# Attention messages moved from VectorE to GpSimd in a graph network on one core

## The chip, the cores and the metric

The kernel runs on one core of a Trainium2 chip. The metric is the device time in microseconds (us). A core has TensorE (PE in the profile), VectorE (DVE), ScalarE (ACT), GpSimd (POOL) and SyncE (SP), which issues DMAs here.

## The reference, cut to what matters

A graph of 12,500 nodes with 32 features and 400,000 edges goes through four layers, each followed by a layer norm: a weighted sum over neighbours, an attention layer, two hops of a normalized sum, and a convolution. The change touches the attention layer:

```python
hp = jnp.einsum('nf,hfo->hno', h, w)             # 4 heads
e = a_src[:, src] + a_dst[:, dst] + fc_b[0]
e = jax.nn.leaky_relu(e, negative_slope=0.2)
seg_max = jax.ops.segment_max(e.T, src, num_segments=n)
e = jnp.exp(e - seg_max.T[:, src])
seg_sum = jax.ops.segment_sum(e.T, src, num_segments=n)
att = e / seg_sum.T[:, src]
msg = att[:, :, None] * hp[:, dst, :]
agg = jax.vmap(lambda m: jax.ops.segment_sum(m, src, num_segments=n))(msg)
out = agg.mean(axis=0) + bias
```

The kernel sums exp(score) times the far node's row, and exp(score) itself (a 33rd column of ones), per source node and head; it divides and projects afterwards. Everything is float32.

## The kernel before, in words

The layers run one after the other as stages; each ends in a barrier of all engines. The attention stage (`attend`) has two paths; the inputs take the bounded one, in which a bound on the scores that was computed earlier takes the place of the maximum. GpSimd's `If` holds only the bounded path.

Edges, sorted by source node, are worked in groups of 512 (128 partitions x `PER` = 4). There are 880 groups in `SRC_PASSES` = 110 turns of `SRC_DEEP` = 8 groups; the first and the last turn are written out and the others are a loop on each engine. Each engine runs its own instruction list, and semaphores tie them. For a group s:

- SP loads the far nodes' rows into `far[s]` (8 buffers, 80 KB each) once `far_free[s]` has been raised.
- VectorE forms `local_node` (L1825, 128x4) and from it `one_hot` (L1830: 512 columns, a comparison of the iota with the local node numbers, both in SBUF).
- TensorE transposes the one-hot (`turn_hot`, L1941); ScalarE copies the result to SBUF (L1983).
- GpSimd copies the node's terms into `b_node` (L2007, 128x8).
- TensorE multiplies the two (`spread_terms`, L1951), which gives each edge its node's terms in PSUM.
- VectorE makes the score in four short operations of 16 columns: `raw_score` (L1836, PSUM and SBUF in), `leaky_score` (L1841, the same SBUF tile as both inputs), `less_bound` (L1845, SBUF and PSUM in), `cap_score` (L1850, SBUF).
- ScalarE takes the exponent into `b_share` (L1987).
- VectorE forms the message (L1855): `far` (33 columns, spread over 4 heads) times `b_share` (spread over 33 columns), both in SBUF, 528 columns out. `free_far` then waits for it and raises `far_free`.
- TensorE sums the messages per node (`sum_nodes`, L1960) into one of two PSUM buffers, and VectorE adds the result to `k.attention` (`accumulate`, L1871).

The work is staggered. In its iteration s VectorE does, in this order: one_hot(s+1), local_node(s+2), messages(s-2), raw_score(s-1), free_far(s-2), leaky_score(s-1), accumulate(s-4), less_bound(s-1), cap_score(s-1). TensorE does turn_hot(s), spread_terms(s-1), sum_nodes(s-3). ScalarE does copy_hot(s), the exponent of s-1. GpSimd only copies node terms, up to four groups ahead (its copy waits for the spread_terms of four groups before). Scores, shares, messages, turned one-hots and node terms have `SLOTS` = 4 buffers each.

Of the kernel before, what the change touches and what calls it, by code (L numbers as in the profile page):

```python
# [20 lines left out]
ALU = mybir.AluOpType  # L21
# [7 lines left out]
HEADS = 4  # L29
# [7 lines left out]
SLOTS = 4  # L37
# [49 lines left out]
SRC_DEEP = 8  # L87
SRC_PASSES = TURNS["by_src"] * SLOTS // SRC_DEEP
# [25 lines left out]
def spread(ap, axis, n):  # L114

    ap = ap.unsqueeze(axis)
    shape = list(ap.shape)
    shape[axis] = n
    return ap.broadcast_to(shape)
# [8 lines left out]
def loop(engine, first, end):  # L128

    return engine.bass.Fori(first, end, engines=[engine.engine], head_slot={engine.engine: 0})  # L130
# [7 lines left out]
def turns(engine, count, one_turn):  # L138

    one_turn(0, True, False)  # L140
    with loop(engine, 1, count - 1) as i:
        one_turn(i, False, False)
    one_turn(count - 1, False, True)
# [1402 lines left out]
def attend(nc, k):  # L1546
# [4 lines left out]
    W = F + 1  # L1551

    def turn(i, slot, of):
        return i * (SRC_DEEP // of) + slot // of + 1

    with stage(nc, k) as ctx:
        def sb(n, shape, dt, count):
            return [ctx.enter_context(nc.sbuf_tensor(f"att_{n}{s}", shape, dt)) for s in range(count)]

        def sem(n, count):  # L1560
            return [k.sem(f"att_{n}{s}") for s in range(count)]

        far = sb("far", [P, PER, FAR], F32, SRC_DEEP)
# [9 lines left out]
        gathered, far_free = sem("gathered", SRC_DEEP), sem("far_free", SRC_DEEP)  # L1573
# [14 lines left out]
        b_share = sb("b_share", [P, PER, HEADS], F32, SLOTS)  # L1588
        b_message = sb("b_message", [P, PER, HEADS * W], F32, SLOTS)
# [7 lines left out]
        b_score_ready, b_share_ready = sem("b_score_ready", SLOTS), sem("b_share_ready", SLOTS)  # L1597
        b_message_ready, b_part_ready = sem("b_message_ready", SLOTS), sem("b_part_ready", SLOTS)
# [216 lines left out]
        def bounded_vector(dve):  # L1815
            steps = Steps(dve, own)
            step, wait = steps.step, steps.wait
            step(dve.memset(k.attention[:], 0.0))
            wait()
            for c in range(2):  # L1820
                dve.sem_inc(part_free[c], 1)

            def local_node(i, s):
                dve.wait_ge(gathered[s % SRC_DEEP], (i + s // SRC_DEEP + 1) * 16)
                return step(dve.tensor_scalar(b_local[s % SLOTS][:], far[s % SRC_DEEP][:, :, SRC_AT],  # L1825
                                              first_node[:, bass.ds(i * SRC_DEEP + s, 1)], None, ALU.subtract))

            def one_hot(s):

                dve.tensor_tensor(b_hot[s % SRC_DEEP][:], spread(k.iota[:], 1, PER),  # L1830
                                  spread(b_local[s % SLOTS][:], 2, P), ALU.is_equal).then_inc(b_hot_ready[s % SLOTS], 1)


            def raw_score(i, s):
                dve.wait_ge(b_terms_spread[s % SLOTS], turn(i, s, SLOTS))
                return step(dve.tensor_tensor(b_score[s % SLOTS][:, 0], b_terms[s % 2][:, :, 0:HEADS],  # L1836
                                              far[s % SRC_DEEP][:, :, W:W + HEADS], ALU.add))

            def leaky_score(s):
                score = b_score[s % SLOTS]  # L1840
                return step(dve.scalar_tensor_tensor(score[:, 1], score[:, 0], 0.2, score[:, 0], ALU.mult, ALU.max))  # L1841

            def less_bound(s):
                score = b_score[s % SLOTS]
                return step(dve.tensor_tensor(score[:, 0], score[:, 1], b_terms[s % 2][:, :, HEADS:2 * HEADS],  # L1845
                                              ALU.subtract))

            def cap_score(s):
                score = b_score[s % SLOTS]
                dve.tensor_scalar(score[:, 1], score[:, 0], 0.0, None, ALU.min).then_inc(b_score_ready[s % SLOTS], 1)  # L1850

            def messages(i, s):
                b = s % SLOTS
                dve.wait_ge(b_share_ready[b], turn(i, s, SLOTS))
                dve.tensor_tensor(  # L1855
                    b_message[b][:].rearrange("p j (h w) -> p j h w", h=HEADS),
                    spread(far[s % SRC_DEEP][:, :, 0:W], 2, HEADS), spread(b_share[b][:], 3, W),
                    ALU.mult).then_inc(b_message_ready[b], 1)

            def free_far(i, s):  # L1860

                dve.wait_ge(b_message_ready[s % SLOTS], turn(i, s, SLOTS))
                dve.sem_inc(far_free[s % SRC_DEEP], 1)

            def bins(first, n):
                return bins_of(nc, mybir.EngineType.DVE, k, "by_src", first, n)

            def accumulate(i, s, at):
                dve.wait_ge(b_part_ready[s % SLOTS], turn(i, s, SLOTS))
                sums = k.attention[:, bass.ds(at * (HEADS * W), HEADS * W)]  # L1870
                return step(dve.tensor_tensor(sums, sums, part[s % 2][:, 0:HEADS * W], ALU.add))  # L1871

            def one_group(i, s, first, last, at, n_local):

                if not (last and s == SRC_DEEP - 1):
                    if n_local:
                        wait(n_local)
                    one_hot(s + 1)
                n_local = None
                if not (last and s >= SRC_DEEP - 2):  # L1880
                    n_local = local_node(i, s + 2)
                if not (first and s < 2):
                    messages(i, s - 2)
                scored = not (first and s < 1)
                if scored:
                    n_raw = raw_score(i, s - 1)
                if not (first and s < 2):
                    free_far(i, s - 2)
                if scored:
                    wait(n_raw)  # L1890
                    n_leaky = leaky_score(s - 1)
                if at is not None:
                    n_added = accumulate(i, s - 4, at)
                if scored:
                    wait(n_leaky)
                    n_less = less_bound(s - 1)
                    wait(n_less)
                    dve.sem_inc(b_terms_read[(s - 1) % SLOTS], 1)
                    cap_score(s - 1)
                if at is not None:  # L1900
                    wait(n_added)
                    dve.sem_inc(part_free[s % 2], 1)
                return n_local

            def one_turn(i, first, last):
                steps.restart()
                at = [None] * 4 + [*bins(0, SRC_DEEP - 4)] if first else bins(i * SRC_DEEP - 4, SRC_DEEP)
                n_local = None
                for s in range(SRC_DEEP):
                    n_local = one_group(i, s, first, last, at[s], n_local)  # L1910
                wait()

            local_node(0, 0)
            wait()
            one_hot(0)
            local_node(0, 1)
            wait()
            turns(dve, SRC_PASSES, one_turn)

            steps.restart()  # L1920
            i, s = SRC_PASSES - 1, SRC_DEEP - 1
            messages(i, s - 1)
            wait(raw_score(i, s))
            wait(leaky_score(s))
            wait(less_bound(s))
            dve.sem_inc(b_terms_read[s % SLOTS], 1)
            cap_score(s)
            at = bins(i * SRC_DEEP + SRC_DEEP - 4, 4)
            for n in range(4):
                wait(accumulate(i, s - 3 + n, at[n]))  # L1930
                dve.sem_inc(part_free[n % 2], 1)
                if n == 0:
                    messages(i, s)

        def bounded_tensor(pe):
            def turn_hot(i, s):
# [60 lines left out]
            exponents(SRC_PASSES - 1, SRC_DEEP - 1)  # L1997

        def bounded_gpsimd(pool):
            def one_turn(i, first, last):  # L2000
                at = bins_of(nc, mybir.EngineType.Pool, k, "by_src", i * SRC_DEEP, SRC_DEEP)
                for s in range(SRC_DEEP):
                    b = s % SLOTS

                    if not (first and s < SLOTS):
                        pool.wait_ge(b_terms_spread[b], turn(i, s, SLOTS) - 1)
                    pool.tensor_copy(b_node[b][:], k.node_terms[:, bass.ds(at[s] * (2 * HEADS), 2 * HEADS)]  # L2007
                                     ).then_inc(b_node_ready[b], 1)

            turns(pool, SRC_PASSES, one_turn)  # L2010

        def bounded(engine):
            return engine.value_load(k.bounded[0:1, 0:1], min_val=0, max_val=1) == 1
# [633 lines left out]
```

## Time and profile before

| what | value |
|---|---|
| median of 3 runs | 25015.46 us (25014.8 to 25022.9) |
| span of the profiled execution | 25016.3 us |
| attention stage, first local_node to last accumulate | 9084.1 to 11346.7 us |
| busy in it: TensorE, VectorE, ScalarE, GpSimd | 2130.6, 1934.4, 629.1, 377.0 us of 2262.0 |

The profiled execution has no other time than its span, which lies 0.8 us above the median of the runs. The page gives busy time per engine over the whole span; since the stages have different limits, the shares that count are those of the attention stage, read from windows and from its timeline.

### The profile page before, as it was taken

Reading aid. Unit: us, or ns where it says so; the run is one execution under the profiler, and the core shown is the slowest. Engines: PE = TensorE matmul, PEld = TensorE weight load, DVE = VectorE, ACT = ScalarE, POOL = GpSimd, SP = SyncE. Lnnn points to the kernel's source line nnn. Section 1 sums busy time; section 2 is a strip of 40 time slices with the busy share of each in tenths; the row PEclk is TensorE's granted clock in tenths of the full one; section 3 lists DMA queues with packets and bytes.
Section 4 is the critical chain, followed back from the end, with each engine's and each line's share of the span. In section 5 each row is a group of like instructions: output and inputs, shape, how many; then the busy total and the mean of one; then the engine's idle time right before and its main releaser. Section 6 shows DMA issues by size and latency. Waiting matters only on the chain. (4 is left out here: it accounts for less than half of the span.)

```text
span 25016.3 us, 315397 instructions
## 1 busy us (share of the span) xinstructions
PE 12737.2 (51%) x63351; PEld 12045.4 (48%) x63352; DVE 12424.7 (50%) x30310; ACT 5405.7 (22%) x16758; POOL 17008.4 (68%) x17867
## 2 busy tenths in 40 slices
PE   0333333344444469994333333333333588888887
PEld 0333333333333359994333333333333577777777
DVE  2377731211111148883222222222222699999999
ACT  6522222200000012220000000000000255555554
POOL 1777777677777741114777776777777677777777
PEclk8555555555555579995555555555555688888888
DMA  1111112332333311110000002000000222222223
GB/s 51 16 16 15 15 17 17 22 70 69 69 69 68 69 45 32 32 32 15 13 13 13 13 13 15 13 13 13 13 13 13 32 43 43 43 43 43 43 43 41
DMA packets 2491356, 794.50 MB, mean 32 GB/s; under 512 B 1959280, under 2 KB 2282065, under 8 KB 2490323
## 3 DMA queue, kind: packets, MB, share of 16 engines
q0 software_dynamic: 517120, 331.99, 9.2%
q1 hardware_dynamic: 1624386, 242.42, 6.0%
q10 hardware_dynamic: 349748, 219.11, 3.5%
q14 instruction: 84, 0.69, 0.0%
q8 instruction: 18, 0.29, 0.0%
HBM read 699.58 MB, written 93.71 MB: 32 GB/s over the span
## 5 line engine op out<-in xcount | busy, mean ns | idle before, releaser
L999 POOL DMA_INDIRECT hop_far<-hop_rows,hop_index x6464 | 6097.5, 943 | 2188.6 <-issue 2188.3
L1061 PE MATMUL hop_part<-hop_far,hop_hot 128*128 128x32 f32 x12928 | 2926.7, 402 | 5268.4 <-DVEq L1046 5268.4
L1061 PEld LDWEIGHTS hop_part<-hop_far,hop_hot 128*128 128x128 f32 x12928 | 2817.9, 330 | 5377.2 <-DVEq L1046 5377.2
L781 POOL DMA_INDIRECT weighted_far<-in_x_dram,weighted_rows x3232 | 3346.7, 1035 | 1505.4 <-issue 980.0
L1131 POOL DMA_INDIRECT rows_by_src<-push_row,push_index x3232 | 3094.7, 958 | 996.3 <-issue 985.0
L2255 POOL DMA_INDIRECT conv_far<-conv_rows x3232 | 3066.4, 949 | 949.9 <-issue 758.5
L1013 DVE TENSOR_TENSOR hop_hot<-hop_iota,local_of_edge 128x1024 f32<-128x1024 f32 x808 | 989.5, 1225 | 5035.4 <-DMA hop_far<-hop_rows,hop_index 3650.2
L2361 PE MATMUL conv_radial_a<-radial,conv_hidden 128*128 128x256 f32 x6464 | 2747.6, 513 | 634.6 <-DVE conv_products_b L2493 566.9
L865 PE MATMUL weighted_total<-weighted_message,weighted_hot 128*128 128x33 f32 x6464 | 1542.8, 404 | 2852.9 <-ACT weighted_message L887 2788.2
L1181 PE MATMUL push_near<-far_rows_sb,push_turned 128*128 x6464 | 1683.6, 436 | 2369.5 <-DVE push_turned L1158 2369.1
L865 PEld LDWEIGHTS weighted_total<-weighted_message,weighted_hot 128*128 128x128 f32 x6464 | 1438.3, 328 | 2958.2 <-issue 2958.2
L1181 PEld LDWEIGHTS push_near<-far_rows_sb,push_turned 128*128 128x128 f32 x6464 | 1569.0, 327 | 2484.0 <-issue 2483.9
L2361 PEld LDWEIGHTS conv_radial_a<-radial,conv_hidden 128*128 128x128 f32 x6464 | 1803.6, 327 | 697.7 <-issue 629.7
L2362 PEld LDWEIGHTS conv_radial_b<-radial,conv_hidden 128*128 128x128 f32 x6464 | 1910.6, 330 | 138.7
L986 ACT COPY hop_index<-source_of_edge 128x8 int32 (+1 forms) x808 | 158.7, 197 | 7965.3 <-PE hop_part L1061 7868.5
L2362 PE MATMUL conv_radial_b<-radial,conv_hidden 128*128 128x128 f32 x6464 | 1781.1, 363 | 0.0
L1166 DVE TENSOR_TENSOR push_index<-push_moved,push_trash 128x4 int32<-128x4 f32 x808 | 132.6, 164 | 3230.6 <-DMA rows_by_src<-push_row,push_index 3229.9
L1021 DVE TENSOR_TENSOR sums<-sums,hop_part 128x32 f32 x6464 | 1213.9, 188 | 923.1 <-issue 94.2
L2007 POOL COPY att_b_node<-node_terms 128x8 f32 x880 | 377.5, 429 | 1893.7 <-PE att_terms_ps L1951 969.9
L2493 DVE TENSOR_TENSOR conv_products_b<-conv_radial_b,conv_pair 128x1536 f32<-128x1536 f32 x808 | 1538.1, 1904 | 0.0
L2410 DVE TENSOR_REDUCE conv_sum_b<-conv_products_b 128x96 f32<-128x1536 f32 x808 | 1531.4, 1895 | 0.0
L887 ACT ACTIVATE weighted_message<-weighted_far,weighted_rows 128x32 f32<-128x32 f32 x3232 | 772.6, 310 | 2627.0 <-DMA weighted_far<-in_x_dram,weighted_rows 2626.8
(256 smaller groups left out, 22490.9 us busy)
## 6 DMA issues: line engine op xcount, KB each, us to landing
push_line<-local_by_group ACTq DMA_DIRECT2D x808, 256.0 KB
hop_far<-hop_rows,hop_index POOLq DMA_INDIRECT x6464
conv_weights<-weight_by_group SPq DMA_DIRECT2D x808, 128.0 KB, 3.0
att_far<-rows_by_src SPq DMA_DIRECT2D x880, 80.0 KB
weighted_far<-in_x_dram,weighted_rows POOLq DMA_INDIRECT x3232, 2.4
push_place<-place_by_dst SPq DMA_DIRECT2D x3232, 0.5 KB
rows_by_src<-push_row,push_index POOLq DMA_INDIRECT x3232
conv_rows<-edges_by_dst SPq DMA_DIRECT2D x3232, 4.0 KB
```

Source lines behind the costliest of these rows:

```text
L781: pool.indirect_dma_start(far[s][:, j, :], None, table, bass.IndirectOffsetOnAxis(ap=rows[s][:, j, 0:1].bitcast(I32), axis=0)).then_inc(ga ...
L865: last = pe.matmul(total[:].rearrange("p n c -> p (n c)")[:, bass.ds(at[s % SLOTS * HALVES + j // COLUMNS], width)], hot[s][:, j, :], mess ...
L999: pool.indirect_dma_start(far[q][:, j, :], None, table, bass.IndirectOffsetOnAxis(ap=index[q][:, j:j + 1], axis=0)).then_inc(gathered[q], 16)
L1021: return steps.step(dve.tensor_tensor(sums, sums, part[q % 2][:, j * F:(j + 1) * F], ALU.add))
L1061: last = pe.matmul(part[q % 2][:, j * F:(j + 1) * F], hot[q][:, j, :], far[q][:, j, :], start=True, stop=True)
L1131: pool.indirect_dma_start(k.rows_by_src, bass.IndirectOffsetOnAxis(ap=index[s][:, j:j + 1], axis=0), row[s][:, j, :], None).then_inc(writt ...
L1181: last = pe.matmul(near[:, b, j * FAR:(j + 1) * FAR], turned[b][:, :, j], k.far_rows[:].rearrange("p b w -> p (b w)")[:, bass.ds(at[b * HA ...
L2255: pool.indirect_dma_start(far[s][:, j, :], None, k.conv_dram, bass.IndirectOffsetOnAxis(ap=rows[s][:, j, 0:1].bitcast(I32), axis=0)).then_ ...
L2361: pe.matmul(radial_a[:, c, j, :], hidden[c][:, :, j], k.radial[:, 0:256], start=True, stop=True)
L2362: last = pe.matmul(radial_b[:, c, j, :], hidden[c][:, :, j], k.radial[:, 256:384], start=True, stop=True)
L2410: return step(dve.tensor_reduce(sum_b[s % 2][:].rearrange("p j o u -> p (j o u)"), products_b[:].rearrange("p j o u m -> p (j o u) m"), AX ...
L2493: dve.tensor_tensor(products_b[:].rearrange("p j o u m -> p (j o u m)"), spread(radial_b[:, c], 2, 3), spread(pair[s][:].rearrange("p j o ...
```

## The change

VectorE no longer forms the messages nor frees the loaded rows. GpSimd does both, in its own iteration s after the copy of the node terms: first free_far(s-3), then messages(s-2). Since VectorE's order no longer protects the message buffer, GpSimd also waits for the sum_nodes that read the buffer four groups before. In VectorE's list the two calls are simply gone; the rest keeps its order.

```diff
--- bounded_vector
-            def messages(i, s):
-                b = s % SLOTS
-                dve.wait_ge(b_share_ready[b], turn(i, s, SLOTS))
-                dve.tensor_tensor(
-                    b_message[b][:].rearrange("p j (h w) -> p j h w", h=HEADS),
-                    spread(far[s % SRC_DEEP][:, :, 0:W], 2, HEADS), spread(b_share[b][:], 3, W),
-                    ALU.mult).then_inc(b_message_ready[b], 1)
-            def free_far(i, s):
-                dve.wait_ge(b_message_ready[s % SLOTS], turn(i, s, SLOTS))
-                dve.sem_inc(far_free[s % SRC_DEEP], 1)
...
-                if not (first and s < 2):
-                    messages(i, s - 2)
...
-                if not (first and s < 2):
-                    free_far(i, s - 2)
--- bounded_gpsimd
+            def messages(i, s, first=False):
+                b = s % SLOTS
+                pool.wait_ge(b_share_ready[b], turn(i, s, SLOTS))
+                if not (first and s < SLOTS):
+                    pool.wait_ge(b_part_ready[b], turn(i, s, SLOTS) - 1)
+                pool.tensor_tensor(
+                    b_message[b][:].rearrange("p j (h w) -> p j h w", h=HEADS),
+                    spread(far[s % SRC_DEEP][:, :, 0:W], 2, HEADS), spread(b_share[b][:], 3, W),
+                    ALU.mult).then_inc(b_message_ready[b], 1)
+            def free_far(i, s):
+                pool.wait_ge(b_message_ready[s % SLOTS], turn(i, s, SLOTS))
+                pool.sem_inc(far_free[s % SRC_DEEP], 1)
             def one_turn(i, first, last):
...
                     pool.tensor_copy(b_node[b][:], ...).then_inc(b_node_ready[b], 1)
+                    if not (first and s < 3):
+                        free_far(i, s - 3)
+                    if not (first and s < 2):
+                        messages(i, s - 2, first)
             turns(pool, SRC_PASSES, one_turn)
+            i, s = SRC_PASSES - 1, SRC_DEEP - 1
+            messages(i, s - 1)
+            messages(i, s)
```

The last two messages, which VectorE formed after its loop, move to the end of GpSimd's list as well.

## Rows read from the trace of the kernel before

**Rows 1.** The page: the span; TensorE's clock in 40 slices, in tenths.

```profile
span 25016.3 us, 315397 instructions
...
PEclk8555555555555579995555555555555688888888
```

**Rows 2.** Windows: us, busy us (count) per engine, TensorE clock, DMA share, GB/s.

```profile
9084.00:11346.00 2262.00, 2130.56 (x17600) 2071.31 (x17600) 1934.41 (x7039) 629.10 (x1761) 376.96 (x876) 0.98 0.13 32
...
9090.00:9100.00 10.00, 10.00 (x49) 10.00 (x48) 6.81 (x24) 2.40 (x7) 0.57 (x3) 0.50 0.09 23
22000.00:22100.00 100.00, 83.30 (x375) 77.81 (x373) 100.00 (x202) 51.33 (x142) 78.02 (x78) 0.87 0.23 43
```

**Rows 3.** Groups by line, stage 9084 to 11346: busy us, mean ns | idle before.

```profile
L1855 DVE TENSOR_TENSOR att_b_message<-att_far,att_b_share 128x528 f32<-128x528 f32 x880 | 616.2, 700 | 0.7 <-ACT att_b_share L1987 0.6
...
L2007 POOL COPY att_b_node<-node_terms 128x8 f32 x876 | 377.0, 430 | 1884.4 <-PE att_terms_ps L1951 969.9 <-PE att_hot_ps L1951 914.5
```

**Rows 4.** Timeline, VectorE: start us, us, engine line op [idle before <-releaser].

```profile
10215.30 0.17 DVE L1850 TENSOR_SCALAR att_b_score<-att_b_score 128x16 f32<-128x16 f32 x1
10216.62 0.69 DVE L1830 TENSOR_TENSOR att_b_hot<-iota,att_b_local 128x512 f32<-128x512 f32 x1 [1.15 <-DVE att_b_score L1845]
...
10219.02 0.69 DVE L1830 TENSOR_TENSOR att_b_hot<-iota,att_b_local 128x512 f32<-128x512 f32 x1
10219.64 0.22 DVE L1825 TENSOR_SCALAR att_b_local<-att_far,first_node_by_src 128x4 f32<-128x4 f32 x1
10219.77 0.69 DVE L1855 TENSOR_TENSOR att_b_message<-att_far,att_b_share 128x528 f32<-128x528 f32 x1
10220.39 0.16 DVE L1836 TENSOR_TENSOR att_b_score<-att_terms_ps,att_far 128x16 f32<-128x16 f32 x1
10220.61 0.17 DVE L1841 SCALAR_TENSOR_TENSOR att_b_score<-att_b_score 128x16 f32<-128x16 f32 x1
10220.76 0.29 DVE L1871 TENSOR_TENSOR attention<-attention,att_part 128x132 f32 x1
10220.97 0.16 DVE L1845 TENSOR_TENSOR att_b_score<-att_b_score,att_terms_ps 128x16 f32<-128x16 f32 x1
10221.28 0.18 DVE L1850 TENSOR_SCALAR att_b_score<-att_b_score 128x16 f32<-128x16 f32 x1
10221.43 0.69 DVE L1830 TENSOR_TENSOR att_b_hot<-iota,att_b_local 128x512 f32<-128x512 f32 x1
```

**Rows 5.** The same, the next turn's first one-hot.

```profile
10237.02 0.69 DVE L1830 TENSOR_TENSOR att_b_hot<-iota,att_b_local 128x512 f32<-128x512 f32 x1 [1.15 <-DVE att_b_score L1845]
```

**Rows 6.** Timeline, TensorE: two groups and the turn's boundary.

```profile
10211.67 0.60 PE L1941 MATMUL att_masked_ps<-ident,att_masked 128*128 128x128 f32 x4
...
10214.01 0.60 PE L1941 MATMUL att_masked_ps<-ident,att_b_hot 128*128 128x128 f32 x4
10214.45 0.96 PE L1951 MATMUL att_hot_ps<-att_b_node,att_b_turned 128*128 128x8 f32 x8
...
10217.37 0.66 PE L1941 MATMUL att_masked_ps<-ident,att_b_hot 128*128 128x128 f32 x4 [0.79 <-DVE att_b_hot L1830]
```

**Rows 7.** Timeline, GpSimd: the node copies.

```profile
10215.57 0.19 POOL L2007 COPY att_b_node<-node_terms 128x8 f32 x1 [1.79 <-PE att_hot_ps L1951]
10218.99 0.19 POOL L2007 COPY att_b_node<-node_terms 128x8 f32 x1 [3.23 <-PE att_terms_ps L1951]
10221.61 0.55 POOL L2007 COPY att_b_node<-node_terms 128x8 f32 x1 [2.44 <-PE att_hot_ps L1951]
```

**Rows 8.** GpSimd's only long elementwise operation: ns min/median/max.

```profile
L2275 POOL TENSOR_TENSOR conv_folded_a<-conv_products_a x808: 1253/1266/1289, 19724.8 to 24968.7; 128x512 f32<-128x512 f32 x162
```

**Rows 9.** Timeline, ScalarE: the share after the capped score at 10221.28.

```profile
10221.49 0.21 ACT L1987 ACTIVATE att_b_share<-att_b_score 128x16 f32<-128x16 f32 x1 [1.72 <-DVE att_b_score L1850]
```

**Rows 10.** Register loads, ns min/median/max, GpSimd's queue.

```profile
L633 POOLq TENSOR_LOAD <-listed x110: 562/566/765, 9070.2 to 11313.1; - x110
```

**Rows 11.** Waits of the DMA queue: us in total, times, longest.

```profile
SPq L1612 <- DVEq L1863: 1679.5, 859, 3.8
```

More of the change, by code:

```diff
@@ L1886, in one_group @@
                     n_raw = raw_score(i, s - 1)
-                if not (first and s < 2):
-                    free_far(i, s - 2)
-                if scored:
                     wait(n_raw)
@@ L1921, in bounded_vector @@
             i, s = SRC_PASSES - 1, SRC_DEEP - 1
-            messages(i, s - 1)
             wait(raw_score(i, s))
@@ L1931, in bounded_vector @@
                 dve.sem_inc(part_free[n % 2], 1)
-                if n == 0:
-                    messages(i, s)
         def bounded_tensor(pe):
```

## The prediction

> **What bounds the kernel now.** I first read the span and the page's slices, which tell where the attention stage lies, by TensorE's clock, which reaches full speed (2.4 GHz) there alone [rows 1]. Windows give the stage 2262 us with TensorE 94% and VectorE 86% busy, GpSimd 17% [rows 2]. So two engines are near their limit, and only the order of instructions tells which one ends last. VectorE's timeline decides it: one group takes 10221.43 - 10219.02 = 2.41 us, and inside a turn VectorE never idles [rows 4]. TensorE needs 10214.01 - 10211.67 = 2.34 us for a group when it runs without a gap [rows 6]. VectorE is the bound by 0.07 us a group only, and at the boundary of each turn it adds 1.15 us of register loads and branch, in which TensorE soon stands too (0.79 us idle) [rows 4, 6]. A turn of eight groups is 10237.02 - 10216.62 = 20.40 us [rows 4, 5]; 110 turns are 2244 us, and the cold start is the rest of the stage.
>
> **What leaves VectorE.** The message is 880 x 0.70 us = 616 us of busy time [rows 3]. From start to start it takes 10220.39 - 10219.77 = 0.62 us out of a group [rows 4], so VectorE alone would need 1.79 us. free_far costs VectorE nothing visible. If nothing else changed, TensorE would be the bound at once, and the most that can be won inside a turn is 0.07 us a group; what more there is lies at the boundary.
>
> **What comes to GpSimd.** Its message is not in the trace. The nearest row is its own 128x512 addition of two SBUF tensors, 1.27 us (1.25 to 1.29) [rows 8]; by columns, 528/512 x 1.27 = 1.31 us. Below, it could be VectorE's 0.70 us [rows 3], above twice the 1.31 (2.6), if the two spread operands cost extra; I take 1.31, the same engine with the same kind of operation. With a node copy of 0.19 us, the waits (it wakes 10215.57 - (10214.45 + 0.96) = 0.16 us behind its releaser [rows 6, 7]) and one register load of 0.57 us a turn [rows 10], GpSimd needs some 1.8 us a group. It has 2.4. By busy time alone nothing speaks against the move.
>
> **What the two engines do to each other.** The node copy takes 0.19 us when VectorE's one-hot isn't under way, but 0.55 us when it starts inside one: started at 10221.61, it ends at 10222.16, 0.04 us after the one-hot that ran from 10221.43 to 10222.12 [rows 4, 7]. Its mean in the stage is 0.43 us [rows 3]. So GpSimd is kept off while VectorE runs an operation with two SBUF inputs. The trace has no case of the reverse, a long GpSimd operation with such a VectorE operation behind it: the only long one runs beside an operation that reads PSUM. I bound the reverse: at least nothing, at most the whole rest of the GpSimd message. I take the whole, since what keeps one engine off for a whole operation looks like one thing that both need, held until the operation ends.
>
> The Trainium skill ("SBUF — State Buffer", section "Who interferes with whom") says the same and more: the port pair that the two share is an exclusive lock, taken for a whole instruction by whoever is first, wanted by a VectorE operation with two SBUF inputs (against a GpSimd operation that reads SBUF) and by the two-port modes, into which fp32 `tensor_scalar` can fall. The trace agrees for one direction (0.55 against 0.19 us); no run here shows the other. By that rule one-hot, leaky_score and perhaps local_node and cap_score would wait for a message, and raw_score, less_bound and accumulate, with one input in PSUM, would not.
>
> **The new cycle, step by step,** counted from the start of cap_score(s-1) [rows 4, 9]:
> - the one-hot starts at 0.15 and ends at 0.15 + 0.69 = 0.84; the share starts at 0.21 and is done at 0.42, so GpSimd finds the message(s-1) ready at about 0.6, inside the one-hot, and is held;
> - held like the copy, the message ends its own length, less the copy's, after the copy would: 0.84 + 0.04 + 1.31 - 0.19 = 2.00;
> - VectorE meanwhile does local_node and raw_score, and wants leaky_score(s) at 0.15 + 1.59 - 0.62 = 1.12. It has two SBUF inputs and must wait to 2.00. It ends between 0.05 and 0.17 later (its latency);
> - cap_score(s) starts 10221.28 - 10220.61 = 0.67 after leaky_score's start, 0.50 after its end: the cycle is 2.55 to 2.67 us;
> - if local_node wants the pair too, it adds up to its own 0.22 us, when it gets in first. Together 2.55 to 2.89 us; I take the middle, 2.72.
>
> The next message can't slip into a better gap, since its share comes only from the cap_score that the one-hot follows at once. So the pattern holds itself: the message falls behind the one-hot and in front of the leaky_score every time.
>
> At a turn's boundary the one-hot comes 10216.62 - 10215.30 = 1.32 after the cap_score [rows 4]. Then the message is first: 0.42 + 0.16 + 1.31 = 1.89, and the one-hot wants its start at 1.32 and waits 0.57. From the one-hot's start to cap_score, without the message, are 10221.28 - 10219.02 - 0.62 = 1.64 us: 1.89 + 1.64 = 3.5 us. GpSimd's own register load falls while it waits for a share.
>
> **Sum.** A turn: 7 x 2.72 + 3.5 = 22.54 us against 20.40, 2.14 more. 110 turns: 235 us. The later stages begin after a barrier, so all of it arrives at the end. On the profiled span: 25016 + 235 = 25251; the median of the runs is 1 us less: 25,250.
>
> **What costs nothing, and its cover.** The wait for the sum of four groups before: that sum lies more than two cycles back. Rows are freed a group later: SP's wait for far_free is what it mostly does (1680 us, longest 3.8) [rows 11], eight buffers still leave three cycles, over 7 us, for a load. accumulate and sum_nodes wait for a message that ends at 2.00, and TensorE wants it after its transposes and its spread of the next iteration, at about 2.3. Should the message be 0.3 us later than that, TensorE's summing would be late next. The scalar engine is unchanged. The two last messages cost about 1 us more, once.
>
> TensorE would have 2.34 us of work in 2.72 (86%). In the convolution, at 83% busy, its clock is granted at 0.87 of full speed [rows 2], against 0.98 here now; at the low level (1.2 GHz) it had no gap left in the stage's start [rows 2]. At 0.87 its group costs 2.34 / 0.87 = 2.69, just under the cycle. I count nothing for it in the middle and up to 0.1 us a group (90 us) in the upper end.
>
> **The rivals.**
> *No blocking of VectorE's operations, faster.* For it: GpSimd's copy at 10218.99 starts 0.03 us before the one-hot and neither is longer for it (0.19, 0.69) [rows 4, 7]; against: an operation of 8 columns may be out by then. Then TensorE is the bound: 8 x 2.34, plus at the boundary 0 to 0.3 us, since VectorE, now 0.6 us a group ahead, hides most of the 1.15. A turn of 18.9 saves 1.5, 110 turns 165 us: 24,850 (24,820 to 24,880). It decides by one thing: whether leaky_score starts before the message ends. With only the one-hot blocked it is the same case, since the VectorE cycle is then about 2.0.
> *The parts cancel.* leaky_score waits only for part of the message, because the message is shorter (below 1.1 us) or lets the 16 columns in. A cycle of 2.35 to 2.48 and a boundary of 3.5 give 20.0 to 20.9 a turn: no change, 25,015.
> *GpSimd becomes the bound.* The spread operands cost extra. Each 0.1 us on the message is 0.1 us on the cycle, 88 us on the kernel; at 2.6 us the cycle is 4.0: some 26,150. Against it: nothing in the row speaks of such a cost; the operands are in SBUF there too.
>
> **Chances.** Forecast (mutual blocking) 0.58; faster rival 0.23; cancelling 0.13; GpSimd the bound 0.06. The forecast's own range is 7 x 2.55 + 3.4 = 21.25 to 7 x 2.89 + 3.6 = 23.8 us a turn, 25,110 to 25,390, with the clock's share up to 25,420. The range over all reaches down into the faster rival, where TensorE's 2.34 sets a floor: 24,835 to 25,420. A change under 0.2% (50 us) can't be told from none here. A little of the forecast's lower end falls under that bound: faster 0.24, same 0.14, slower 0.62.
>
> **What would show it.** GpSimd's L2007 mean and its new message group: about 1.3 us alone, near 1.5 from its start where it begins inside a one-hot. VectorE: idle time or a longer duration at leaky_score (0.9 us a group), none at raw_score. One-hots 2.7 us apart and 3.5 at the boundary. TensorE idle 0.3 to 0.4 us a group and a granted clock under 0.98. The forecast is wrong if VectorE's waits sit on raw_score behind TensorE's spread (the faster rival), or if GpSimd shows no gap at all.

## The result, and the profile after

The changed kernel takes 25220.16 us (median of 4 runs, 25216.36 to 25225.3) against 25015.13 us, a ratio of 1.0081 (95% interval 1.0067 to 1.0096): slower by 205 us, where 235 us had been forecast. Its profiled execution has a span of 25223.6 us. The number is close, but by luck: the cost that the forecast was made of came to a third of its size, the clock, which it had put at nothing, cost more than that, and a third part wasn't foreseen.

The page after, its span and TensorE's granted clock in 40 slices, and three windows (columns as in [rows 2]): the attention stage, a usual turn of it, and a slow one:

```profile
span 25223.6 us, 316380 instructions
...
PEclk8555555555555579996555555555555688888888
```

```profile
9117.00:11555.00 2438.00, 2245.12 (x17600) 2182.38 (x17600) 2036.28 (x6160) 631.91 (x1761) 1272.46 (x1757) 0.93 0.12 29
10229.00:10250.00 21.00, 19.01 (x162) 18.36 (x160) 18.43 (x56) 5.58 (x16) 11.53 (x17) 1.00 0.13 31
10250.30:10275.90 25.60, 24.67 (x160) 24.48 (x160) 18.73 (x57) 6.08 (x16) 11.57 (x17) 0.73 0.10 26
```

The stage goes from 2262.6 us (9084.1 to 11346.7) to 2438.0 us, 175 us more. TensorE's clock in it falls from 0.98 to 0.93, and the third window shows where: a turn of 25.6 us with a clock of 0.73, in which TensorE is busy for 24.67 us, so it hardly waits. Of the 109 intervals from a turn's first one-hot to the next, 82 are about 21.07 us and 27 are 24.3 to 26.2 us. Before, most were 20.40 us and the others 20.7, but for the first, with the cold start in it (25.8).

The groups of the stage (columns as in [rows 3]), and VectorE's and GpSimd's timelines of one cycle, beside [rows 4]:

```profile
L1984 POOL TENSOR_TENSOR att_b_message<-att_far,att_b_share 128x528 f32<-128x528 f32 x880 | 1105.9, 1257 | 1174.1 <-ACT att_b_share L1966 1174.0
L1825 DVE TENSOR_SCALAR att_b_local<-att_far,first_node_by_src 128x4 f32<-128x4 f32 x880 | 835.5, 949 | 0.2 <-DVE attention L1818 0.2
...
L2001 POOL COPY att_b_node<-node_terms 128x8 f32 x877 | 212.6, 242 | 2.3 <-issue 2.3
```

```profile
10201.72 0.17 DVE L1850 TENSOR_SCALAR att_b_score<-att_b_score 128x16 f32<-128x16 f32 x1
10201.86 0.69 DVE L1830 TENSOR_TENSOR att_masked<-iota,att_b_local 128x512 f32<-128x512 f32 x1
10202.47 1.05 DVE L1825 TENSOR_SCALAR att_b_local<-att_far,first_node_by_src 128x4 f32<-128x4 f32 x1
10203.44 0.16 DVE L1836 TENSOR_TENSOR att_b_score<-att_hot_ps,att_far 128x16 f32<-128x16 f32 x1
10203.64 0.17 DVE L1841 SCALAR_TENSOR_TENSOR att_b_score<-att_b_score 128x16 f32<-128x16 f32 x1
10203.76 0.29 DVE L1858 TENSOR_TENSOR attention<-attention,att_part 128x132 f32 x1
10203.97 0.17 DVE L1845 TENSOR_TENSOR att_b_score<-att_b_score,att_hot_ps 128x16 f32<-128x16 f32 x1
10204.28 0.17 DVE L1850 TENSOR_SCALAR att_b_score<-att_b_score 128x16 f32<-128x16 f32 x1
10204.43 0.69 DVE L1830 TENSOR_TENSOR att_b_hot<-iota,att_b_local 128x512 f32<-128x512 f32 x1
```

```profile
10202.22 1.28 POOL L1984 TENSOR_TENSOR att_b_message<-att_far,att_b_share 128x528 f32<-128x528 f32 x1 [1.15 <-ACT att_b_share L1966]
10203.44 0.19 POOL L2001 COPY att_b_node<-node_terms 128x8 f32 x1
```

VectorE's local_node, 4 columns wide, took 0.22 us before and takes 1.05 us now. It starts at 10202.47, while the message runs, and ends at 10203.52, 0.02 us after the message (10202.22 + 1.28 = 10203.50). raw_score and leaky_score behind it have their usual lengths. The message itself is held too: its 1.28 us began inside the one-hot. It is so in the whole stage: 768 of the 880 local_nodes start inside a message, take 1.06 us (median) and end 0.02 to 0.03 us after it; the others take 0.22 us. From cap_score to cap_score the cycle is 10204.28 - 10201.72 = 2.56 us; it was 2.41.

A turn's boundary, VectorE first, then GpSimd:

```profile
10206.84 0.17 DVE L1850 TENSOR_SCALAR att_b_score<-att_b_score 128x16 f32<-128x16 f32 x1
10208.17 0.89 DVE L1830 TENSOR_TENSOR att_b_hot<-iota,att_b_local 128x512 f32<-128x512 f32 x1 [1.16 <-DVE att_b_score L1845]
...
10209.95 0.17 DVE L1850 TENSOR_SCALAR att_b_score<-att_b_score 128x16 f32<-128x16 f32 x1
...
10229.23 0.89 DVE L1830 TENSOR_TENSOR att_b_hot<-iota,att_b_local 128x512 f32<-128x512 f32 x1 [1.16 <-DVE att_b_score L1845]
```

```profile
10207.43 1.08 POOL L1984 TENSOR_TENSOR att_b_message<-att_far,att_b_share 128x528 f32<-128x528 f32 x1 [1.23 <-ACT att_b_share L1966]
```

Here VectorE is busy with its registers when the share is ready. The message starts with VectorE out of its way, takes 1.08 us to 10208.51, and now it is the one-hot (from 10208.17) that is longer, 0.89 in place of 0.69 us. From cap_score to cap_score these are 3.11 us, and the turn is 10229.23 - 10208.17 = 21.06 us.

TensorE in the slow turn, the first transposes of four groups (columns as in [rows 6]):

```profile
10255.41 1.06 PE L1920 MATMUL att_masked_ps<-ident,att_b_hot 128*128 128x128 f32 x4
...
10259.73 1.06 PE L1920 MATMUL att_masked_ps<-ident,att_b_hot 128*128 128x128 f32 x4
...
10269.04 0.60 PE L1920 MATMUL att_masked_ps<-ident,att_masked 128*128 128x128 f32 x4
...
10271.27 0.60 PE L1920 MATMUL att_masked_ps<-ident,att_masked 128*128 128x128 f32 x4
```

At the low clock level (1.2 GHz) a group takes 10259.73 - 10255.41 = 4.32 us, TensorE back to back. When the level returns to 2.4 GHz it catches up, still without a gap, at 10271.27 - 10269.04 = 2.23 us a group. This is its true floor; the 2.34 us of [rows 6] wasn't. Besides the one that the stage starts in, the record of the clock has 26 low stretches in the stage both before and after, but of 3.4 us each before (89 us in all) and of 10.2 or 13.7 us now (338 us).

Ahead of the stage lies one more difference. GpSimd's indirect DMAs there, before and after (ns min/median/max):

```profile
L1131 POOL DMA_INDIRECT rows_by_src<-push_row,push_index x3232: 954/958/1005, 4981.8 to 9060.8; - x191
```

```profile
L1131 POOL DMA_INDIRECT rows_by_src<-push_row,push_index x3232: 965/969/1013, 4979.0 to 9093.6; - x191
```

11 ns more for each of 3232, in a stage whose code is the same: 36 us, of which 33 arrive at the attention stage (9116.9 - 9084.1), since the first of these DMAs comes 3 us earlier. So the 207 us between the spans are 33 ahead of the stage, (21.07 - 20.40) x 110 = 74 us of longer cycles, and the remaining 101 us of slow turns, beyond what such turns cost before.

### The profile page after: what moved, and what is told of

Read it like the earlier page. It is cut to its first block and busy times, and to the rows that moved or that the text cites. A ratio compares the mean times of both kernels' runs of the same rounds, so it can differ in the third digit from the quotient of the medians.

```text
span 25223.6 us, 316380 instructions
## 1 busy us (share of the span) xinstructions
PE 12847.3 (51%) x63351; PEld 12154.6 (48%) x63352; DVE 12526.2 (50%) x29430; ACT 5409.5 (21%) x16758; POOL 17938.9 (71%) x18747
## 5 line engine op out<-in xcount | busy, mean ns | idle before, releaser
L1984 POOL TENSOR_TENSOR att_b_message<-att_far,att_b_share 128x528 f32<-128x528 f32 x880 | 1105.9, 1257 | 1174.1 <-ACT att_b_share L1966 1174.0
```

## The experiments

In the first eight runs of the table the kernel before takes 27,400 to 27,660 us, since the stages of indirect DMAs are longer there, before and after alike: the one ahead of attention takes 4803 us from its first to its last such DMA in before_again, for 4079 us in the trace before. The cause isn't known, and it isn't the chip as such: by the record fill_tensor ran on the chip of the first four, at 25,120 us. The attention stage isn't longer (2260.4 us in before_again). So these runs are compared by their ratio to the kernel before in the same series, and by the length of the attention stage; the microseconds of their expectations are to be read as differences from 25,015. The 11 ns cost nothing in them (4800 us in after_again, 4803 in before_again), so their ratios lack the 33 us.

| run | ratio (95% interval) | stage, us | usual turn, us | low clock, us |
|---|---|---|---|---|
| before_again | one run | 2260.4 | 20.40 | 92 |
| after_again | one run, +171 us | 2429.7 | 21.06 | 311 |
| local_first | 1.0034 (1.0021 to 1.0048) | 2365.7 | 20.71 | 256 |
| psum_ops_first | 0.9908 (0.9892 to 0.9925) | 2019.5 | 18.27 | 0 |
| after_psum | 0.9897 (0.9880 to 0.9913) | 1979.4 | 17.86 | 0 |
| before_psum | 0.9999 (0.9989 to 1.0009) | 2261.8 | 20.38 | 113 |
| psum_order | 0.9894 (0.9877 to 0.9910) | 1984.6 | 17.86 | 7 |
| half | 1.0002 (0.9992 to 1.0011) | 2256.8 | 20.43 | 0 |
| local_psum | 0.9902 (0.9885 to 0.9918) | 1979.3 | 17.86 | 0 |
| free_only | 0.9999 (0.9989 to 1.0009) | 2262.6 | 19.97 | 195 |
| pad | one run, -2 us | 2260.2 | 20.40 | 96 |
| fill_tensor | 1.0043 (1.0030 to 1.0057) | 2327.3 | 21.05 | 10 |

The stage runs from the first local_node's start to the last accumulate's end, the usual turn is the median from one turn's first one-hot to the next, and the low clock is the sum of the stretches at the low level in the stage, without the one of 13 to 26 us that it starts in.

**after_again and before_again: do the parts repeat?**

> The changed kernel once more, unchanged. Its trace showed three parts of the 207 us: cycles of 2.56 us instead of 2.40 (73 us), a turn of 25.6 us instead of 21.1 about every fourth turn, in which TensorE's clock is at its low level for 13.7 us (some 100 us), and 36 us in the stage before attention, where each of GpSimd's 3232 indirect DMAs takes 11 ns longer from start to start (1.274 against 1.263 us). Theory: all three belong to the kernel and repeat: span 25,205 to 25,235, the stage before at 1.274 us, about 26 low stretches of 10 to 14 us. Rival: the slow turns and the 11 ns are chance of one execution; then one or both are gone (25,080 to 25,190).

> The kernel before once more, unchanged. If the 11 ns belong to the change, GpSimd's indirect DMAs of the stage before attention stand at 1.263 us again; if they are chance of an execution, they may stand at 1.274. Low stretches of TensorE's clock: 26 of 3.4 us as before, turns of 20.40 us with 20.7 every third or fourth.

They do: 1.274 and 1.263 us from one indirect DMA to the next (median), 24 low stretches of 10 to 14 us against 26 of mostly 3.4 us, turns of 21.06 and 20.40 us. The whole difference, 171 us, is less than the 190 to 220 expected; 169 of it lie in the attention stage.

**local_first: what else is held?** The edit, in VectorE's list (cut to the calls; their waits move with them):

```diff
-                    one_hot(s + 1)
-                    n_local = local_node(i, s + 2)
+                    n_local = local_node(i, s + 2)
+                    one_hot(s + 1)
```

> The changed kernel with local_node(s+2) ahead of one_hot(s+1) in VectorE's list; then no operation with a single SBUF input stands between one-hot and leaky_score. Theory (whatever VectorE operation next wants the shared pair is held): local_node falls back to 0.22 us and leaky_score (two SBUF inputs, 16 columns) is held for about 0.8 us; cycle 0.28 + 0.69 + 0.04 + 1.08 - 0.19 + 0.05 + 0.50 = 2.45 us, turn about 20.5 without the slow turns, 25,060 to 25,160. Rival (only local_node is ever held, 16 columns slip in): nothing is held, TensorE is the bound at 2.34 us, turn about 19.0, some 24,880.

The two groups of VectorE that matter, from a part of the stage:

```profile
L1841 DVE SCALAR_TENSOR_TENSOR att_b_score<-att_b_score 128x16 f32<-128x16 f32 x556 | 387.3, 697 | 19.0
...
L1825 DVE TENSOR_SCALAR att_b_local<-att_far,first_node_by_src 128x4 f32<-128x4 f32 x556 | 127.5, 229 | 144.7 <-issue 106.7
```

local_node is back at 0.23 us, and leaky_score, 16 columns from two SBUF inputs, goes from 0.18 to a mean of 0.70 us (median 0.86). The usual cycle is 2.50 us (2.45 expected), and the ratio of 1.0034 is inside what the theory gave. The rival, that only local_node is ever held, is out.

**psum_ops_first: an order that runs beside the message.** The calls alone, again:

```diff
                     one_hot(s + 1)
-                    n_local = local_node(i, s + 2)
                     n_raw = raw_score(i, s - 1)
+                    n_added = accumulate(i, s - 4, at)
                     n_leaky = leaky_score(s - 1)
-                    n_added = accumulate(i, s - 4, at)
                     n_less = less_bound(s - 1)
+                    n_local = local_node(i, s + 2)
                     cap_score(s - 1)
```

> The changed kernel with VectorE's list reordered: after one_hot come raw_score and accumulate (one input in PSUM each), then leaky_score, less_bound, local_node, cap_score. Theory: the message (ends 1.64 us after the one-hot's start in the changed kernel) now runs beside the two operations that don't want the pair; leaky_score ends at 1.7 to 1.8, cap_score starts at about 2.1, the next one-hot at 2.25; TensorE's 2.34 us is the bound, turns of 19.0 to 19.5 us, no long low stretches of the clock: 24,870 to 24,950. Rival (the hold doesn't depend on which operands are in PSUM, only on GpSimd being busy): raw_score is held as local_node was, cycle 2.5 or more, 25,150 to 25,230.

```profile
L1841 DVE SCALAR_TENSOR_TENSOR att_b_score<-att_b_score 128x16 f32<-128x16 f32 x653 | 334.3, 512 | 0.0
...
L1858 DVE TENSOR_TENSOR attention<-attention,att_part 128x132 f32 x652 | 189.2, 290 | 0.0
...
L1836 DVE TENSOR_TENSOR att_b_score<-att_terms_ps,att_far 128x16 f32<-128x16 f32 x326 | 57.0, 175 | 33.3 <-PE att_terms_ps L1931 29.1
```

raw_score and accumulate, which read one input from PSUM, keep their lengths (0.18 and 0.29 us) though 767 and 768 of them start inside a message; leaky_score behind them is held, but for less (mean 0.51 us). VectorE's usual cycle is 2.17 us. That the ratio, 0.9908, lies under the expected 0.994 to 0.997 comes mainly from TensorE, which needs 2.23 and not 2.34 us a group: the turn is 18.27 us for an expected 19.0 to 19.5, some 80 us over 110 turns.

**after_psum, before_psum, local_psum: take away the need for the shared pair.** The turned one-hots use two PSUM banks instead of four (`s % 2`); the bank that is free takes the local node numbers, in the first two kernels the output of less_bound as well:

```diff
+        near = [masked_ps[:, 3, n * PER:(n + 1) * PER] for n in range(SLOTS)]
...
-                return step(dve.tensor_scalar(b_local[s % SLOTS][:], far[...], ...))
+                return step(dve.tensor_scalar(near[s % SLOTS], far[...], ...))
...
-                                  spread(b_local[s % SLOTS][:], 2, P), ALU.is_equal)
+                                  spread(near[s % SLOTS], 2, P), ALU.is_equal)
```

> The changed kernel, its order kept, with the local node numbers and the output of less_bound in a spare PSUM bank (the turned one-hots use two banks in place of four). Then one_hot, local_node and cap_score have at most one operand in SBUF that they read and write through the shared pair; only leaky_score still has two SBUF inputs. Theory (the shared pair is the cause): one-hot and local_node aren't held, the message starts inside the one-hot at once (0.6 us after cap_score) and ends at 1.7, leaky_score is held some 0.5 us; cycle at or under TensorE's 2.34, turns 19.0 to 19.6, 24,860 to 24,950. Rival (GpSimd's work as such holds VectorE): local_node still about 1 us, cycle 2.56 or more, 25,200 or more.

> The same move to PSUM in the kernel before, messages on VectorE. It shows what the move itself is worth. Theory: GpSimd's node copy goes from 0.55 to 0.19 us where it starts in a one-hot and is held only by a message; VectorE stays the bound at 2.41 us or a little over, for reading PSUM; 25,010 to 25,100. Rival (the move itself makes VectorE faster): 24,950 or less.

> The changed kernel with only the local node numbers in the spare PSUM bank; less_bound and cap_score stay in SBUF as before. Theory: what the changed kernel lost came from local_node (fp32 tensor_scalar, SBUF to SBUF) held behind the message, and from the message held behind the one-hot; both end here, and the attention stage is as with both moved (1979 us, turns of 17.9 us): about 0.990 of the kernel before. Rival (cap_score matters as much): between the changed kernel and that, a turn of 19 us or more.

local_psum, VectorE, then GpSimd's message in the same cycle, and a window over most of the stage:

```profile
10202.17 0.69 DVE L1835 TENSOR_TENSOR att_masked<-iota,att_masked_ps 128x512 f32<-128x512 f32 x1
10202.77 0.22 DVE L1830 TENSOR_SCALAR att_masked_ps<-att_far,first_node_by_src 128x4 f32<-128x4 f32 x1
10203.40 0.17 DVE L1841 TENSOR_TENSOR att_b_score<-att_terms_ps,att_far 128x16 f32<-128x16 f32 x1 [0.41 <-PE att_terms_ps L1935]
10203.61 0.17 DVE L1846 SCALAR_TENSOR_TENSOR att_b_score<-att_b_score 128x16 f32<-128x16 f32 x1
...
10204.40 0.69 DVE L1835 TENSOR_TENSOR att_masked<-iota,att_masked_ps 128x512 f32<-128x512 f32 x1
```

```profile
10202.52 1.09 POOL L1989 TENSOR_TENSOR att_b_message<-att_far,att_b_share 128x528 f32<-128x528 f32 x1 [0.88 <-ACT att_b_share L1971]
```

```profile
9150.00:11050.00 1900.00, 1900.00 (x17024) 1900.00 (x17023) 1449.19 (x5955) 645.96 (x1702) 1046.83 (x1703) 1.00 0.15 37
```

The message starts at 10202.52, inside the one-hot, and isn't held: 1.09 us. Nor are the one-hot (0.69) and local_node (0.22, while the message runs). VectorE's wait is now at raw_score, for TensorE, which is busy for all of 1900 us at the full clock. A turn is 17.86 us, 8 x 2.23. In before_psum the same move changes nothing in the time (0.9999), but GpSimd's node copy falls from 0.43 [rows 3] to 0.22 us:

```profile
L2013 POOL COPY att_b_node<-node_terms 128x8 f32 x840 | 186.8, 222 | 1963.5 <-PE att_terms_ps L1957 996.8 <-PE att_hot_ps L1957 966.8
```

The copies that start inside a one-hot take 0.19 us there for 0.55 before. So the move as such isn't what gains; it gains since neither engine holds the other any longer. local_psum does as well as after_psum (1979.3 and 1979.4 us): one tile in PSUM is enough, and cap_score didn't matter. after_psum, at 0.9897, came out under its range (0.994 to 0.997), again by TensorE's 2.23 us. psum_order adds the order to it:

> Both: the operands in PSUM and the order in which raw_score and accumulate come before leaky_score. Theory: nothing of note is held on either engine, TensorE is the bound, turns of 18.8 to 19.2 us: 24,840 to 24,900, the same or up to 50 us better than either alone. Rival (the boundary of the turn stays at 3.1 us and isn't hidden): 24,950.

It is the same within the intervals, and under its own range (0.993 to 0.995) for the same reason; TensorE is the bound already. The boundary is hidden, so the rival is out.

**half: does a hold last as long as GpSimd's operation?** GpSimd forms heads 0 and 1, VectorE heads 2 and 3 after local_node. GpSimd's part of the edit:

```diff
-                    spread(far[...][:, :, 0:W], 2, HEADS), spread(b_share[b][:], 3, W),
+                    spread(far[...][:, :, 0:W], 2, 2), spread(b_share[b][:, :, 0:2], 3, W),
```

> The changed kernel with the message divided: GpSimd forms heads 0 and 1, VectorE heads 2 and 3 after its local_node. Theory (a hold lasts as long as GpSimd's operation): GpSimd's part takes 0.15 + 0.93/2 = 0.62 us, ends 0.84 + 0.04 + 0.62 - 0.19 = 1.31 after cap_score, VectorE's part adds 0.35, cycle 1.31 - 0.06 + 0.35 + 0.20 + 0.64 = 2.44 us: near the kernel before, 25,020 to 25,100. Rival (a hold has a fixed price, whatever the length): 0.83 us of hold stays, cycle about 2.9, 25,400 or more.

```profile
L1999 POOL TENSOR_TENSOR att_b_message<-att_far,att_b_share 128x264 f32<-128x264 f32 x842 | 678.9, 806 | 1149.8 <-ACT att_b_share L1981 1149.8
...
L1834 DVE TENSOR_SCALAR att_b_local<-att_far,first_node_by_src 128x4 f32<-128x4 f32 x842 | 468.0, 556 | 0.0
...
L1827 DVE TENSOR_TENSOR att_b_message<-att_far,att_b_share 128x264 f32<-128x264 f32 x842 | 354.7, 421 | 0.0
```

```profile
10450.00:12600.00 2150.00, 2020.00 (x16836) 1943.82 (x16835) 1874.34 (x6736) 591.51 (x1682) 972.20 (x1684) 1.00 0.13 32
```

By their means, GpSimd's half takes 0.81 us with its hold (1.26 for the whole) and local_node 0.56 us (0.95). The 768 local_nodes that start inside a message take 0.60 us (1.06) and again end 0.03 us after it. The cycle is 2.45 us where 2.44 was worked out, and the time is that of the kernel before. A hold lasts until the operation that holds has ended.

**fill_tensor: are the slow turns the clock's?**

```diff
+                    for n in range(2):
+                        pe.transpose(masked_ps[:, 3, n * P:(n + 1) * P], k.ident[:], k.ident[:])
```

> The changed kernel with two more transposes of a constant tile per group on TensorE, written to a spare PSUM bank that nobody reads (the turned one-hots use two banks in place of four); VectorE and GpSimd keep their order and hold each other as before. TensorE then has some 2.45 us of work in a cycle of 2.56. Theory (the 25.6 us turns come from TensorE's clock, which falls since TensorE now has gaps): the long low stretches go or shrink to 3.4 us, the usual turn stays at 21.07, the attention stage goes from 2430 to 2438 us to about 2330 to 2350; with the 36 us of the stage before, 1.004 to 1.006 of the kernel before. Rival (the slow turns have another cause, TensorE's clock follows them): they stay, 1.007 to 1.009, or more for the added work.

A window of fill_tensor (the kernel before has its own in [rows 2], the changed kernel further up):

```profile
9150.00:11300.00 2150.00, 2049.28 (x17942) 1982.10 (x17942) 1879.28 (x5708) 574.54 (x1632) 1181.07 (x1631) 1.00 0.13 31
```

More work on TensorE makes the kernel faster than the changed one: the stage goes from 2438.0 to 2327.3 us, 111 us less and 3 us under the range given, and the ratio from 1.0081 to 1.0043, in its range. The usual turn is unchanged at 21.05 us, and the slow turns are gone but for one low stretch of 10 us.

**free_only and pad: the small parts.** free_only is the kernel before with free_far alone on GpSimd; pad is the kernel before with 160 instructions in the branch that isn't taken.

> The kernel before with free_far alone moved to GpSimd; the messages stay on VectorE. Theory: freeing the rows a group later from GpSimd costs nothing in the attention stage: cycles 2.40, turns 20.40, stage 2258 to 2266 us. Of the stage before it: if any waits and semaphore instructions more in GpSimd's program bring the 11 ns, its DMAs are 1.274 us apart (36 us, ratio 1.0013); if it is the elementwise operation, they stay at 1.263.

> The kernel before with 160 instructions that do nothing in the branch of GpSimd's program which the inputs never take. It asks whether the 11 ns per indirect DMA in the stage before attention come from how long GpSimd's program is, or where its parts lie: then 1.274 us or another value than 1.263. If it stays at 1.263, the place of code isn't the cause.

VectorE in free_only, two one-hots behind a boundary, 2.34 us apart, where before they are 2.41 [rows 4]:

```profile
10303.37 0.69 DVE L1830 TENSOR_TENSOR att_b_hot<-iota,att_b_local 128x512 f32<-128x512 f32 x1 [1.16 <-DVE att_b_score L1845]
...
10305.71 0.69 DVE L1830 TENSOR_TENSOR att_b_hot<-iota,att_b_local 128x512 f32<-128x512 f32 x1
```

Taking free_far off VectorE does shorten its usual cycle, to 2.35 us, and the usual turn to 19.97 us, which wasn't expected; 110 x 0.43 = 47 us should be won. Nothing is: the low clock stretches grow from 89 to 195 us and the stage stays at 2262.6. The indirect DMAs are 1.266 and 1.263 us apart in free_only and pad. In the same execution of free_only, those of the hop stage are 1.251 us apart instead of 1.249, so 2 ns of it are that execution's. The 11 ns come with neither the length of the program nor a few more waits; they came in each kernel whose GpSimd forms messages.

## Why the prediction was right, by its own steps

- **Mutual holding: right, and the cause of the loss in the cycle.** It was inferred from one direction, and both are now shown: a VectorE operation with two SBUF inputs and the fp32 local_node wait until the GpSimd operation has ended (after, local_first, half), and those with an operand in PSUM don't (psum_ops_first, local_psum). At the turn's boundaries it is the one-hot that starts inside a message: 0.89 us with both inputs in SBUF (after), 0.69 us with one in PSUM (local_psum). The rule of the Trainium skill ("SBUF — State Buffer", section "Who interferes with whom") holds here in both directions. That it is a pair of ports that they wait for is the page's account; the runs show who is held, how long, and what ends it.
- **Which operation is held: wrong.** The step said leaky_score, with local_node as an extra of up to 0.22 us when it gets in first. local_node doesn't get in first. The message has the pair as soon as the one-hot lets go, so local_node is held, and leaky_score stands behind it. From the message's end to the next cap_score are 10204.28 - 10203.50 = 0.78 us, against the 0.55 to 0.67 (middle 0.61) counted for leaky_score, or 0.72 with the middle of the extra. This decides more than it seems: with the message's true length (1.08 us, below) the step's own sum for leaky_score gives 1.77 + 0.61 = 2.38 us, the cycle of the rival in which the parts cancel (2.35 to 2.48, with a message below 1.1 us). The rival's condition came true; that the cycle still grew is local_node's doing.
- **The message's own time: mis-sized.** 1.31 us by columns from [rows 8]; it is 1.08 us where nothing holds it. With 1.08, the step's sum for its end is 0.84 + 0.04 + 1.08 - 0.19 = 1.77 us after cap_score, and 1.78 is measured. The spread operands cost nothing extra; if anything they are cheaper than those of that row, which aren't spread. Cycle: 2.56 for 2.72; boundary: 3.11 for 3.5; the turn 21.06 for 22.54. The longer cycles therefore cost 74 us and not 235, less than the forecast's own lower end (21.25 us a turn, 94 us).
- **The clock: its price was put at nothing in the middle, 90 us at most.** It cost about 101 us, the largest part of the loss. (The range's upper end, 25,420, holds 30 of those 90 us only: 25,390 + 90 is 25,480.) fill_tensor shows it: TensorE kept occupied, 111 us come back. The step had compared TensorE's work at a mean clock with the mean cycle; but a low stretch of 13.7 us can't be averaged away. In it a group takes 4.32 us against a cycle of 2.56, and every group behind it waits.
- **33 us outside the stage** were in no step, and their cause is open.
- So 74 + 101 + 33 stands in the place of 235. The direction, and the kind of holding that the cycle turns on, were right; that the sum came within 30 us is luck, a term three times too large against two that were put at nothing.
- **"TensorE needs 2.34 us": wrong.** It was read from two starts while VectorE paced TensorE, and the timeline showed no gap. But from the spread's start to the sum's lie 0.89 us there and 0.81 us in the catch-up after, and the sum itself is a little longer:

```profile
10212.11 0.96 PE L1951 MATMUL att_terms_ps<-att_b_node,att_b_turned 128*128 128x8 f32 x8
10213.00 1.17 PE L1960 MATMUL att_part<-att_b_message,att_masked 128*128 128x132 f32 x8
```

```profile
10269.48 0.96 PE L1930 MATMUL att_hot_ps<-att_b_node,att_b_turned 128*128 128x8 f32 x8
10270.29 1.15 PE L1939 MATMUL att_part<-att_b_message,att_b_hot 128*128 128x132 f32 x8
```

The floor is 2.23 us, and the faster rival was priced too low for it: a kernel without the holding gains 247 us (local_psum, 24765.15 against 25011.74), where the rival said 165. Its attention stage gains 283 us; its DMAs of the stage before have the 11 ns too.
- **"free_far costs VectorE nothing visible": wrong by 0.05 us a group.** Freed rows a group later cost nothing, as said.
- **The price of the last rival: wrong, without effect.** At a cycle of 4.0 us, 1.28 us over the forecast's 2.72, 880 groups cost some 1130 us on top of 25,250: about 26,380, not 26,150. GpSimd didn't become the bound.

## What to carry to other kernels

Before work moves from VectorE to GpSimd, list for each VectorE operation whether it reads two SBUF operands, or is an fp32 SBUF-to-SBUF `tensor_scalar`. Here each such one waited until the GpSimd operation that ran, with its inputs in SBUF, had ended, so a 4-column operation can cost a microsecond; what stands in VectorE's list just behind the operation that the GpSimd work queues for is what pays. One operand in PSUM (for the `tensor_scalar`, its output), or an order that puts PSUM readers there, took this same move from 0.8% slower to 1% faster. And where TensorE is near its limit, read the lengths of its low clock stretches and not the mean clock: shortening another engine's work by 0.05 us a group won nothing (free_only), and lengthening TensorE's own won 100 us (fill_tensor).

## What the runs showed of the hardware that was not expected

- An fp32 `tensor_scalar` of 128x4 from SBUF to SBUF is held until a GpSimd operation ends (1.05 us for 0.22); written to PSUM it isn't (0.22 us).
- GpSimd multiplies 128x528 fp32, both operands spread, in 1.08 us, and adds 128x512 from two operands that aren't spread in 1.27 us [rows 8]; why isn't tested. The Trainium skill ("GPSIMD Engine Reference", section "Performance versus the Vector engine") gives about 2.6 cycles an element for two inputs, which at its 1.2 GHz is an estimate of 1.14 us for 528 without any dispatch; the spread case is below that.
- The same share of TensorE's time went with different clocks: half has it busy for 2020 of 2150 us and no low stretch, the kernel before for 94% too [rows 2] and 26 of them. What sets the length of a low stretch (3.4, 6.8, 10.2 or 13.7 us) isn't settled by these runs.
- GpSimd's indirect DMAs of an unchanged stage are 11 ns longer in every kernel whose GpSimd has the message in its program; neither more waits nor a longer program did it. They cost 33 us where these DMAs follow each other evenly (1.26 us apart in the mean) and nothing where the stage was longer (1.49 to 1.51 us in the mean). The cause is open.
